# Last image of a spectral block kernel: bias products of tiles 0 and 1 moved around the first transform's second half, output tiles interleaved with the second products

## What is computed

```python
def conv(x):                                   # x is normalized before (_gn)
    bias = x @ bias_w.T + bias_b               # 384 x 384, per pixel
    xf = rfftn(x.reshape(B, H, W, 4, 96), axes=(1, 2), norm='ortho')
    xr, xi = xf.real, xf.imag
    r1 = relu(xr @ w1[0] - xi @ w1[1] + b1[0]) # block-wise, 4 blocks of 96
    i1 = relu(xr @ w1[1] + xi @ w1[0] + b1[1])
    r2 = r1 @ w2[0] - i1 @ w2[1] + b2[0]
    i2 = r2 @ w2[1] + i1 @ w2[0] + b2[1]
    return irfftn(complex(r2, i2), s=(H, W), norm='ortho').reshape(B, H, W, C) + bias
x = x + conv(_gn(x))                           # _gn: group norm, 32 groups of 12 channels
```

## Time and profile before

| | |
|---|---|
| median of 3 runs | 426.53 us (425.56 to 427.38) |
| profiled execution | 424.55 us, span 422.7 us |
| PE busy | 392.5 us (93%) |
| DVE busy | 289.6 us (68%) |
| ACT busy | 228.7 us (54%) |
| POOL busy | 167.5 us (40%) |

### The profile page before, as it was taken

The page is one execution under the profiler, slowest core; times in us unless marked ns, Lnnn a source line. Parts: engine busy times, 40 slices in busy tenths (PEclk is TensorE's granted clock), DMA queues, the critical chain, the costliest instruction groups (busy, mean ns, idle before and its releaser), DMA issues.

```text
span 422.7 us, 19391 instructions
## 1 busy us (share of the span) xinstructions
PE 392.5 (93%) x8578; PEld 323.9 (77%) x8578; DVE 289.6 (68%) x728; ACT 228.7 (54%) x514; POOL 167.5 (40%) x114
## 2 busy tenths in 40 slices
PE   3369799999999999999999999999999999998996
PEld 3367689887887878788787878788787988876794
DVE  4797677874687557865678657865578747877525
ACT  2884766356752676447662667436663567426420
POOL 0000001990049600992039800793019900699200
PEclk9859999999999999999999999999999999999999
DMA  6670000180003500170002600062001800040004
GB/s 219 184 256 4 2 3 4 40 299 3 3 17 147 182 3 4 40 283 20 3 4 105 236 3 5 29 227 86 3 5 40 301 3 3 18 174 3 5 3 151
DMA packets 12407, 32.98 MB, mean 78 GB/s; under 512 B 4962, under 2 KB 6660, under 8 KB 12324
## 3 DMA queue, kind: packets, MB, share of 16 engines
q1 hardware_dynamic: 12324, 31.74, 21.2%
HBM read 16.00 MB, written 12.58 MB: 68 GB/s over the span
## 4 chain that ended last, share of the span: by engine, by line
PE 86%; ACT 5%; DVE 4%; issue 2%; DMA 1%; DVEq 0%; SPq 0%; ACTq 0%
PE bank L576 86%; DVE rho L1047 2%; DMA x_sb<-in_x 1%; ACT rho L969 1%; ACT y L930 1%; ACT junk L918 1%; ACT yraw L910 1%; ACT r L940 1%; ACT biasw L944 1%; DVE o_sb L1142 0%; ACT w2s L944 0%; DVE r L1126 0%; ACT z L950 0%; ACT junk L921 0%; DVE w1R L1047 0%
## 5 line engine op out<-in xcount | busy, mean ns | idle before, releaser
L576 PE MATMUL bank<-biasw,yt 128*64 128x384 f16 x1008 | 92.6, 327 | 0.0
L576 PE MATMUL bank<-w2s,rho 128*64 128x96 f16 x3072 | 84.9, 207 | 0.0
L882 POOL TENSOR_TENSOR x_sb<-x_sb,added 128x384 f32<-128x384 f32 x8 | 8.0, 1001 | 192.1 <-DVE yraw L1113 192.1
L576 PEld LDWEIGHTS bank<-w2s,rho 128*64 128x64 f16 x3072 | 80.0, 109 | 5.3 <-issue 2.5
L892 POOL COPY yt<-y 128x1024 f16<-128x1024 f16 x42 | 84.1, 2059 | 0.0
L884 POOL TENSOR_TENSOR x_sb<-x_sb,added 128x384 f32<-128x384 f32 x56 | 74.6, 1364 | 0.0
L576 PEld LDWEIGHTS bank<-biasw,yt 128*64 128x64 f16 x1008 | 54.0, 110 | 20.2 <-issue 0.3
L576 PE MATMUL bank<-w1R,y 128*128 128x192 f16 (+3 forms) x768 | 60.3, 228 | 5.4 <-ACT y L930 3.4
L1047 DVE SCALAR_TENSOR_TENSOR rho<-bank,rho 128x256 f16<-128x256 f32 (+2 forms) x128 | 40.2, 365 | 32.1 <-ACT rho L969 18.6
L950 ACT ACTIVATE z<-bank 128x384 f16<-128x384 f32 x72 | 35.3, 490 | 49.0 <-PE bank L576 48.1
L576 PE MATMUL bank<-tab,x_sb 128*128 128x128 f32 x384 | 50.5, 287 | 8.1 <-DMA x_sb<-in_x 6.5
(11 more groups left out here) (116 smaller groups left out, 474.6 us busy)
## 6 DMA issues: line engine op xcount, KB each, us to landing
x_sb<-in_x SPq DMA_DIRECT2D x16, 768.0 KB, 7.2
out<-o_sb SPq DMA_DIRECT2D x14, 768.0 KB, 4.0
y<-y SPq DMA_DIRECT2D x24, 128.0 KB, 2.7
out<-o_sb SPq DMA_DIRECT2D x8, 192.0 KB, 1.9
tab<-in_tab SPq DMA_DIRECT2D x1, 672.0 KB, 6.3
o_sb<-in_bias_wt SPq DMA_DIRECT2D x4, 144.0 KB, 2.8
b1raw<-in_b1h SPq DMA_DIRECT2D x1, 384.0 KB, 6.6
g<-in_w2t SPq DMA_DIRECT2D x2, 144.0 KB, 2.6
```

The source lines that it names most:

```text
L576: return nc.tensor.matmul(o, lhsT, rhs, start=start, stop=stop, **kw)
L882: nc.gpsimd.tensor_tensor(tiles[:, 0, :], tiles[:, 0, :], added[:, 0, :], ALU.add).then_inc(x_shifted, 1)
```

## The change

It concerns the last image alone. The bias product of tile 1 moves ahead of `p3_half(1)` and reads `y` with a step of eight elements; that of tile 0 moves from behind `p3_last` to ahead of j = 1; that of tile 2 stays ahead of j = 4; that of tile 3 moves from the loop over tiles to ahead of j = 7, with a wait for the low part of j = 5. In the loop the output tile gi - 2 follows `c2_rho(gi)` for gi = 2 to 6, and only tiles 5, 6 and 7 are left behind the last one. DVE's adds move to the matching places.

```diff
--- before.py
+++ after.py
@@ -709,12 +709,10 @@
 
 
                 for j in range(8):
-                    if j in (2, 4, 7):
-                        gi = {2: 0, 4: 1, 7: 2}[j]
-                        if more:
-                            c2_bias(b, p, gi, more, first)
-                        elif gi:
-                            c2_bias(b, p, 3 - gi, more, first)
+                    if more and j in (2, 4, 7):
+                        c2_bias(b, p, {2: 0, 4: 1, 7: 2}[j], more, first)
+                    elif not more and j in (1, 4, 7):
+                        c2_bias(b, p, {1: 0, 4: 2, 7: 3}[j], more, first)
                     if j == 0:
                         pe.wait_ge(rl_ready, 9 * b + 6)
                     elif j == 1 and more:
@@ -757,14 +755,17 @@
                                               r[:, of, 8, at:at + last_row - first_row], xi[:, w, 96 * ri:96 * ri + 96], of == 0 and w == 0 and tile in (0, 1) and first_row == 64 * tile, of == 1, skip_group_check=True)
                     last.then_inc(rho_prod, 1)
 
-            def c2_bias(b, p, gi, more, first, cts=range(NT)):
+            def c2_bias(b, p, gi, more, first):
 
                 if first and gi == 0:
                     pe.wait_ge(bias_ready, 1 + NT)
                 if gi == 0 and not more:
                     pe.wait_ge(rl_ready, 9 * b + 4)
                 elif gi == 1 and not more:
-                    pass
+                    pe.wait_ge(o_ready, 8 * b + 8)
+                elif gi == 3 and not more:
+                    pe.wait_ge(rhoh_ready, 8 * b + 6)
+                    pe.wait_ge(rhol_ready, 8 * b + 6)
                 elif gi < 3:
                     pe.wait_ge(rl_ready, 9 * b + 7 + gi)
                 else:
@@ -773,10 +774,11 @@
                 if gi == 0 and not first:
                     pe.wait_ge(yt_ready, 2 * NT * b)
                 bank = g_bank(gi, more)
-                for ct in cts:
+                in_order = first or (gi == 1 and not more)
+                for ct in range(NT):
                     for of, w in ((0, 0), (0, 1), (1, 0)):
                         for part in range(2):
-                            columns = y[p][:, of, ct, part, gi:512:8] if first else yt[:, of, ct, part, 64 * gi:64 * gi + 64]
+                            columns = y[p][:, of, ct, part, gi:512:8] if in_order else yt[:, of, ct, part, 64 * gi:64 * gi + 64]
                             mm(bank[64 * part:64 * part + 64, 0:CH], columns, biasw[:, w, ct, :],
                                ct == 0 and of == 0 and w == 0, False, skip_group_check=True)
 
@@ -818,25 +820,27 @@
                     if more:
                         p1(b + 1, 1 - p, m)
                     if m == 0:
+                        if not more:
+                            c2_bias(b, p, 1, more, first)
                         p3_half(b, 1, first)
                     if m == 2:
                         p3_last(b)
-                    if not more and m > 2:
-                        c2_bias(b, p, 0, more, first, cts=[m - 3])
                 p4(b, p, more, first)
                 pe.wait_ge(rhoh_ready, 8 * b + 7)
                 pe.wait_ge(rhol_ready, 8 * b + 7)
                 for gi in range(8):
-                    if gi >= 3:
+                    if gi >= (3 if more else 4):
                         c2_bias(b, p, gi, more, first)
-                    if gi == 7:
+                    if gi == 7 and more:
                         p6(b, range(EARLY))
                     c2_rho(b, gi, more, first)
+                    if not more and 2 <= gi < 7:
+                        p6(b, [gi - 2])
                     if gi == 1 and more:
                         mean(b + 1)
                     if gi == 3 and more:
                         variance(b + 1)
-                p6(b, range(EARLY, TILES))
+                p6(b, range(EARLY if more else 5, TILES))
 
             pe.wait_ge(width_in, 16)
             for m in range(Y_ITEMS):
@@ -1194,11 +1198,16 @@
                 for gi in range(4, 7):
                     if more:
                         y_low(b + 1, 1 - p, gi - 4)
+                    else:
+                        add_x(b, p, gi - 4)
                     g_low(b, gi, more)
-                for t in range(EARLY):
+                if not more:
+                    add_x(b, p, 3)
+                    add_x(b, p, 4)
+                for t in range(EARLY if more else 0):
                     add_x(b, p, t)
                 g_low(b, 7, more)
-                for t in range(EARLY, TILES):
+                for t in range(EARLY if more else 5, TILES):
                     add_x(b, p, t)
 
             nc.vector.memset(w1raw[:, :, :, :], 0.0).then_inc(w1_zeroed, 1)
```

## The result

The changed kernel took 427.7 us (median of 14 runs, 426.2 to 429.31), the kernel before 425.7 (14 runs, 424.63 to 428.02). The ratio is 1.004, with a 95% interval of 1.0024 to 1.0057: slower by 0.4%. The interval lies on both sides of the 0.5% line.

What follows compares the result with a forecast made beforehand. PE was taken to bound the kernel, with DVE setting the end. First second product +2.90, loop +0.45 and end -1.08 sum to +2.27 us; on the median of 426.53 that gave 428.8 us, range 426.8 to 430.4.

Steps and rivals of the forecast that it cites:

- Tile 1 ahead of the second half: Its bias product, 1.67 us from `y`, fills PE's idle 0.69 us ahead of `p3_half(1)`, which moves by +0.91 us.
- j = 0: Without tile 0's bias product ahead of this row, PE idles 0.90 us there and the row starts 0.23 us later.
- `p4`: From j = 0 to the first second product: three bias products, two open round trips; 11.06 us against 8.39, +2.67.
- The loop: Loop over tiles loses one bias product (-1.46) and a three-tile block (-1.69), gains five single output tiles (3.60): +0.45 us.
- The end: Behind the last low part stand three DVE adds and not five: -1.08 us.
- queued stores: After the last add, stores had held each other up; up to 0.5 us more won: +1.77, 428.3 us; chance 0.12.
- evictions that keep up: In `p4`, j = 3 and tile 3 find their banks read, without new idle times: -0.16, 426.4 us; chance 0.08.
- free switches: In the loop, single output tiles cost 0.52 us each, nothing for switching: +1.27, 427.8 us; chance 0.12.
- a fall of the clock: PE's three idle times lower its clock, 3 us at half speed losing 1.5 us: 430.3 us; chance 0.05.

Runs made afterwards that it cites:

- the kernels with tile 0 and tile 3 back: Changed kernel with tile 0's bias product back behind `p3_last` (ratio 1.0023 to the kernel before); separately, changed kernel with tile 3's back in the loop (1.0038).
- the kernel with output tiles alone: The kernel before, with only the change's loop of single output tiles and its adds, bias products unmoved; ratio 1.0011 to the kernel before.
- The kernel in pairs: Changed kernel with output tiles 0 to 4 in three blocks (two pairs and one single) in place of five; ratio 1.0053 to the kernel before.
- the kernel with thirds: The kernel before, with bias products of tiles 0 to 2 cut into thirds and put where PE idled; ratio 0.9975 to the kernel before.
- the kernel with a third ahead of j = 5: Against the kernel with thirds, tile 2's last two thirds moved ahead of j = 5 and j = 7; ratio 0.9983 to the kernel before.

## Why the prediction was right

Step by step, from the rows above:

- **Tile 1 ahead of the second half:** forecast +0.91. Measured: the second half starts 387.92 - 385.60 = 2.32 us into the stretch, before 1.41: +0.91, and the length of the bias product from `y` is 1.74 again. The gap was filled, but with a product longer than the gap. No run moves tile 1 by itself; its part is read from these rows.
- **j = 0:** forecast +0.23, measured 390.66 - 385.60 = 5.06 against 4.85, +0.21. The idle time opened where tile 0 had stood (0.81; forecast 0.90).
- **`p4`:** forecast +2.67, so that the first second product comes 2.90 later; measured 16.07 - 13.24 = +2.83. The idle times of 1.21 and 1.27 are those forecast (1.22 and 1.21). That they come from splitting the pair of j = 0 and 1, and from round trips that lie open there with or without tile 3, is shown by the kernels with tile 0 and tile 3 back. From j = 0 on it is 16.07 - 5.06 = 11.01 us, forecast 11.06.
- **The loop:** forecast +0.45. From tile 0's high part to tile 7's it took 420.79 - 404.22 = 16.57 us; before 416.52 - 400.38 = 16.14 (the row of tile 0 before is below): +0.43. The price of 0.72 for one output tile, which no row showed, held, and the kernel with output tiles alone has the same. The kernel in pairs gives its parts: 0.49 for the tile, 0.23 for the block. The forecast had them as 0.59 with the switch out, and 0.13 for the switch in.
- **The end:** forecast -1.08, measured 2.73 - 3.78 = -1.05.

```profile
400.38 0.49 ACT L935 ACTIVATE g<-bank 128x384 f16<-128x384 f32 x1 [1.96 <-PE bank L576]
```

Of the rivals, queued stores are out (2.38 us behind the last add against 2.40), so are evictions that keep up (the two idle rows), free switches (0.72 us for one output tile, 0.23 of it for the block) and a fall of the clock (the windows). The rule of the Trainium skill on frequent short idling (TensorE: Matmul & The Clock Gate, A second HAM failure mode) finds no case here; PE idled three times within ten us at an unchanged grant of 1.00.

Only the last step was loose: set against the median of three runs (426.53) the sum gave 428.8. With 14 runs that median is 425.7, and the difference of the medians is 2.0 us, so the absolute time came out 1.1 us lower, inside the range; 0.8 us of that is the lower median of before, which is chance and not the mechanism. Slower by over 0.5% was given 0.52; the measured 0.4% lies on the other side of that line, though its interval reaches across. A stretch of known +2.2 us is as close to the line as the sum had said.

## What to carry to other kernels

An idle time that one engine shows is not free room of its own length: look at what the moved work covered where it stood, and whether in its new place it splits two instructions whose evictions ran as a pair. Work fits into a round trip only up to its length, so cut it into pieces of that size; here thirds of a product won where whole products lost. Pulling instructions out of a block of their kind costs a switch in and a switch out each time, here 0.23 us together, and moving work from a tail that DVE sets (0.54 us a tile) to a loop that PE sets (0.49 a tile and the switch) wins nothing.

## What the runs showed of the hardware that was not expected

DVE's copy of float16 within SBUF took 0.24 us, but 0.76 in the kernel with thirds, where a tensor add of GpSimd had 0.66 us left to run when the copy started; delaying the adds brought 0.24 back and 0.43 us of the stretch. In the kernel with a third ahead of j = 5 the add had 0.71 us left and the copy took 0.81:

```profile
392.50 0.81 DVE L1181 COPY rho<-rho 128x288 f16<-128x288 f16 x1
386.47 6.74 POOL L886 TENSOR_TENSOR x_sb<-x_sb,added 128x384 f32<-128x384 f32 x7
```

In the kernel before, the add had only 0.14 us left, and the copy took its usual 0.24:

```profile
393.61 0.24 DVE L1179 COPY rho<-rho 128x288 f16<-128x288 f16 x1
390.85 2.90 POOL L884 TENSOR_TENSOR x_sb<-x_sb,added 128x384 f32<-128x384 f32 x3
```

In all three the copy ends 0.10 us behind the add. DVE's evictions, which read PSUM, kept their 0.72 beside such adds. The Trainium skill (SBUF — State Buffer, Who interferes with whom) states that copies can take a port pair that DVE shares with GpSimd, and that whoever comes second then waits for the other's whole instruction; the copy's end 0.10 us behind the add's in each of the three agrees.

The second thing is a part of the scatter between executions. PE's timeline of the kernel before shows three rows in images 1, 3 and 5 (counted from 0) that waited for nothing that the profile shows:

```profile
95.38 0.32 PE L576 MATMUL bank<-w1R,y 96*32 96x96 f16 x7 [0.85 <-issue]
...
192.21 0.31 PE L576 MATMUL bank<-w1R,y 96*32 96x96 f16 x5 [0.56 <-issue]
...
289.04 0.30 PE L576 MATMUL bank<-w1R,y 96*32 96x96 f16 x3 [0.55 <-issue]
```

The changed kernel, whose instructions are the same up to there, has the same three:

```profile
95.17 0.31 PE L576 MATMUL bank<-w1R,y 96*32 96x96 f16 x7 [1.45 <-issue]
...
192.30 0.31 PE L576 MATMUL bank<-w1R,y 96*32 96x96 f16 x5 [0.84 <-issue]
...
290.02 0.30 PE L576 MATMUL bank<-w1R,y 96*32 96x96 f16 x3 [1.43 <-issue]
```

They sum to 1.96 and 3.72 us, a difference of 1.76; ahead of the first of them the changed kernel was 0.81 us sooner, and 1.00 us of later start remained in the last image. All eleven traces have these waits at the same place of `c1`, within a few matmuls, and their sum lies between 1.96 and 3.72 us. They are not all of the scatter: PE comes to the first of them between 93.26 and 95.71 us. What these waits are was not tried; they stay open.
